# Reordering every engine's instruction sequence, and shortening the buffer rings, in a two-phase adaLN block (selective scan, then two local-attention layers)

## The chip, the cores and the metric

The program runs on one core of a Trainium2 chip. The metric is the device time of one execution in microseconds (us). The kernel before takes 4263.51 us, the median of three executions (4262.46 to 4267.74). The engines of the core are TensorE (PE, whose weight loads are shown apart as PEld), VectorE (DVE), ScalarE (ACT) and GpSimd (POOL); SyncE (SP) only issues transfers here.

## The reference

Input are 16 sequences of 512 tokens by 256 features. The block does two things to each, one behind the other:

```python
h = layernorm(x) * (1 + ca) + sa
xz = h @ W_in.T;  x_ssm, z = split(xz)                 # 2 x 512 features
B = x_ssm @ W_B.T;  C = x_ssm @ W_C.T                  # 16 states
dt = softplus(x_ssm @ W_dt.T + b_dt)
state = exp(dt * A) * state + dt * B * x_ssm           # per feature and state, over 512 tokens
y = (sum over states of state * C) + x_ssm * D
x = x + ga * ((y * silu(z)) @ W_out.T) * sigmoid(gate)
h = layernorm(x) * (1 + cb) + sb
for layer in (0, 1):   # input and output are h
    q, k, v = shift_token(h) @ wqkv[layer]             # 8 heads of 64
    q, k = rotary(l2norm(q) * qs, l2norm(k) * ks)
    h = h + local_attention(q, k, v, window=128) @ wo  # own and previous window
    u = layernorm(shift_token(h)) * lg + lb
    a, g = split(u @ w1 + b1)
    h = h + (a * gelu(g)) @ w2 + b2
out = x + gb * h
```

## The kernel before

**Two phases.** The first, the mixer (tiles with names `a_`), handles the 16 sequences one by one. The second, the stack (names `b_`), makes 32 passes, layer 0 for the 16 sequences and then layer 1.

**The mixer.** The 512 inner features are four blocks of 128 partitions (d = 0 to 3), the 16 states are eight groups of two. One unit is one group of one block, so there are 32 units per sequence, and a tile of a unit has 128 x 1024 float32 (two states by 512 tokens). Units 0 to 15 belong to d = 0 and 1 (even units to d = 0), units 16 to 31 to d = 2 and 3 (even units to d = 2). A unit passes through these steps: `decay` (ACT, L684: the exponential), `bcast` (PE, L565: B spread over partitions into one of two slots; needed for 22 units, whose input DVE makes), `mul` (DVE L737 for those 22, POOL L806 for the other 10), `scan` (DVE, L755), `cmul` (POOL, L813: times C), `sum` (PE, L573: added up in one of two PSUM banks, `a_y_sum0` for even units and `a_y_sum1` for odd). When the last sum of a block is there, `gate` (DVE, L761) reads the bank. `gate` of d = 2 needs sum 30, `gate` of d = 3 needs sum 31, and `skip` (PE, L554) then begins the two banks anew. `bcast` and a `decay` into a slot wait for the scan two units earlier, which read that slot (a `bcast` 1 waits for scan 31 of the sequence ahead). Projections come from PE (L524: `xs`, `z`, `bc`, `dt`), `zcopy` (ACT, L634) clears the bank of `z`. The tiles with C come by DMA (SP, L462): load k fills a ring slot and waits until the products of the pair of units that held that slot are done.

**The stack.** Per pass: q, k and v (PE L1296), norms (ACT L1459 to L1468, DVE L1669 to L1680), rotary (`prot`: POOL L1601 for the cosine half, DVE L1695 for the sine half; `padd` DVE L1701), then per window w (0 to 3) and half `score` (PE L1346), `mask` (DVE L1728, whose second half ends with the row bias, L1734), `exp` (ACT L1506), `rate` (DVE L1745), `pn` (POOL L1628), `pt` (PE L1357 and its copies, DVE L1741 or ACT L1518), `att` (PE L1373), `onorm` (DVE L1759), and then `wo`, layernorm (`add` L1766 and L1770, `cen` L1785, `xn` L1790, `hns` L1652), `ga` (PE L1407), `gelu` (ACT), `gated` (DVE L1802), `hh` (ACT L1571), `hl` (the low part of the hidden values: POOL L1635 for blocks 0 to 4, DVE L1751 for block 5), `wd` (PE L1428, block by block) and `fin` (DVE L1807).

**What sets the order.** No scheduler runs. Each phase has one table of steps: `MIXER_ORDER` (L139) and `ORDER` (L829). An entry `name:i` is step `name` of unit, window or block i; a suffix `-` or `+` shifts it to the sequence before or behind. Each engine goes through the table and carries out, in that order, those steps that it owns (`pipeline`, L433 and L1129); semaphores do the rest. So the table's relative order of two steps of one engine is that engine's order. `BANK_OF` (L842) says which of eight PSUM banks holds each product of the stack. The four constants in L33 are the depths of the rings for decays, states, C tiles and B tiles.

Of the kernel before, what the change touches and what calls it, by code (L numbers as in the profile page):

```python
# [144 lines left out]
bload:9 sum-:15 bcast-:19 dt-:0 zcopy-:3 bcast-:20 cload:3 mul-:19 scan-:16 cmul-:16 skip-:1 decay-:30 bcast-:21
scan-:17 gate-:0 bclow-:0 scan-:18 cload:4 decay-:31 sum-:16 decay:0 sum-:17 bcast-:22 gate-:1 silu-:0 sum-:18
cmul-:17 cmul-:18 scan-:19 mul-:20 bcast-:23 mul-:21 scan-:20 decay:1 soft-:1 scan-:21 mul-:22 sum-:19 bcast-:24
decay:2 sum-:20 bcast-:25 decay:3 cmul-:19 cmul-:20 cload:5 z-:0 z-:1 cmul-:21 mul-:23 decay:4 stat:0 mul-:24 mul-:25
decay:5 decay:6 scan-:22 norm:0 cmul-:22 scan-:23 xcopy:0 cmul-:23 sq2:0 cmul-:24 cmul-:25 sum-:21 z-:2 cmul-:26
x1store:0 bcast-:26 decay:7 z-:3 mod:0 bcast-:27 sum-:22 scan-:24 scan-:25 up:0 mul-:26 sum-:23 cload:6 bcast-:28  # L150
mul-:27 cmul-:27 scan-:26 scan-:27 decay:8 sum-:24 bcast-:29 mul-:28 sum-:25 mul-:29 sum-:26 bcast-:30 mod:1 up:1
sum-:27 scan-:28 bcast-:31 cload:7 scan-:29 dt-:1 mul-:30 sum-:28 cload:8 bcast:0 dtadd-:0 sum-:29 bcast:1 mul-:31
sum-:30 decay:9 cmul-:28 scan-:30 cload:9 scan-:31 cmul-:29 sum-:31 bload:12 decay:10 decay:11 cmul-:30 dev2:0 mul:0
skip:0 scan:0 mul:1 xcopy:1 out:0 bcast:2 gate-:2 gate-:3 xscopy:0 scan:1 decay:12 bcast:3 cload:10 scan:2 h2store:0
# [1883 lines left out]
```

How the kernel before makes its waits and increments, by code:

```python
    def wait_free(self, eng, s, name):  # L81
        n = self.at[name]
        _, bank, lead, *_ = self.uses[n]
        for back, held in ((0, self.uses[:n]), (-1, self.uses), (-2, self.uses)):
            found = [use for use in held if use[1] == bank and self.happens(use, s - lead + back + use[2])]
            if found:
                name, _, before, _, _, released, k = found[-1]
                eng.wait_ge(released.sem, released.at(s - lead + back + before - self.since.get(name, 0), k))
                break
# [1 line left out]
    def wait_full(self, eng, s, name):  # L92
        _, _, _, full, k, _, _ = self.uses[self.at[name]]
        eng.wait_ge(full.sem, full.at(s - self.since.get(name, 0), k))
# [105 lines left out]
    def wait_free(self, eng, s, name):  # L201
        at = next(n for n, use in enumerate(self.uses) if use[0] == name)
        turn = s - self.uses[at][2]
        until = {}
        for bank in self.uses[at][1]:
            for back in (0, -1, -2):
                held = self.uses[:at] if back == 0 else self.uses
                found = [use for use in held if bank in use[1] and self.happens(turn + back + use[2])]
                if found:
                    _, _, lead, signal, k = found[-1]
                    until[signal] = max(until.get(signal, (back + lead, k)), (back + lead, k))
                    break
        for signal, (back, k) in until.items():
            eng.wait_ge(signal.sem, signal.at(turn + back, k))
```

## Time and profile before

| | |
|---|---|
| median of three executions | 4263.51 us |
| the profiled execution | 4263.51 us, span 4261.7 us |
| PE busy | 4046.0 us (95%) |
| DVE busy | 3709.7 us (87%) |
| POOL busy | 2694.5 us (63%) |
| ACT busy | 2678.9 us (63%) |
| last step of the mixer's sequences at | about 1725 us |

The span lies 1.8 us inside the profiled execution's time, and that execution is the median one. Busy shares are means over both phases: the mixer fills about the first 1725 us, the stack the rest.

### The profile page before, as it was taken

The numbers are of one execution on the slowest core, as the hardware profiler recorded it, in microseconds if no ns is written. First come the engines' busy times: TensorE is split into PE (matmuls) and PEld (weight loads), VectorE is DVE, ScalarE is ACT, GpSimd is POOL, SyncE is SP. The second block draws the span as 40 slices with busy tenths as digits, with TensorE's granted clock in tenths as the row PEclk, the third lists the DMA queues.
The fourth block names the chain that finished last, engine by engine and source line by source line (L and its number), as shares of the span: only waits on it lengthen the run. The fifth ranks groups of instructions, "written<-read, shape, count | busy, mean of one in ns | idle before, by whom it ended". The sixth has DMA issues, their size and how long they took to land.

```text
span 4261.7 us, 60079 instructions
## 1 busy us (share of the span) xinstructions
PE 4046.0 (95%) x19614; PEld 2631.5 (62%) x19614; DVE 3709.7 (87%) x5981; ACT 2678.9 (63%) x5767; POOL 2694.5 (63%) x1297
## 2 busy tenths in 40 slices
PE   7999999999999998569999999999999999999997
PEld 4444444444444443357777777777777777777775
DVE  5999999999999999568888888888888888888884
ACT  6776767777766775236566565656656565665654
POOL 3999999999999999344444343444434344443442
PEclk8999999999999999779999999999999999999999
DMA  3333333333333333320000000001110101001000
GB/s 112 115 119 124 120 128 123 127 119 120 124 123 126 119 122 111 108 92 21 26 21 16 31 16 27 20 26 55 53 45 25 32 26 32 30 26 36 21 31 25
DMA packets 118499, 295.02 MB, mean 69 GB/s; under 512 B 21208, under 2 KB 43664, under 8 KB 118192
## 3 DMA queue, kind: packets, MB, share of 16 engines
q1 hardware_dynamic: 116320, 291.15, 20.5%
q8 instruction: 160, 2.62, 0.3%
q14 instruction: 147, 1.20, 0.1%
q10 hardware_dynamic: 1872, 0.05, 0.0%
...
## 4 chain that ended last, share of the span: by engine, by line
PE 50%; DVE 5%; ACT 1%; issue 1%; DMA 1%; POOL 0%; SPq 0%; DVEq 0%
PE b_bank L1296 12%; PE b_bank L1407 12%; PE b_bank L1286 5%; PE b_bank L1373 5%; PE b_bank L1346 5%; PE b_bank L1357 4%; PE b_bank L1428 3%; PE b_bank L1326 3%; DVE b_h_part L1751 2%; DVE b_qk L1680 1%; PE b_bank L1387 1%; PE b_bank L1392 1%; DVE b_probs_t L1741 0%; DVE b_qk_rot L1695 0%; ACT b_probs_t L1518 0%
## 5 line engine op out<-in xcount | busy, mean ns | idle before, releaser
L813 POOL TENSOR_TENSOR a_state<-a_state,a_c_wide 128x1024 f32<-128x1024 f32 x512 | 1195.1, 2369 | 19.5 <-DVE a_state L755 19.5
L573 PE MATMUL a_y_sum<-a_state,a_ident 128*128 128x512 f32 x2048 | 951.4, 597 | 6.8 <-POOL a_state L813 6.8
L1628 POOL TENSOR_TENSOR b_scores<-b_scores,b_row_rate 128x1024 f32<-128x1024 f32 (+1 forms) x256 | 455.4, 1800 | 726.1 <-DVE b_row_rate L1745 726.1
L755 DVE TENSOR_TENSOR_SCAN a_state<-a_decay,a_slot 128x1024 f32<-128x1024 f32 x352 | 788.6, 2270 | 0.7
L1296 PE MATMUL b_bank<-b_w_qkv,b_hx_part 128*128 128x512 f32 x2304 | 634.1, 418 | 34.7 <-DVE b_w_qkv L1830 16.6
L573 PEld LDWEIGHTS a_y_sum<-a_state,a_ident 128*128 128x128 f32 x2048 | 387.3, 191 | 383.2 <-issue 316.9
L1601 POOL TENSOR_TENSOR b_by_cos<-b_qk,b_rotary 128x1024 f32<-128x1024 f32 x128 | 352.9, 2757 | 377.4 <-DVE b_qk L1680 375.4
L1506 ACT ACTIVATE b_scores<-b_scores,b_row_bias 128x256 f32<-128x256 f32 (+1 forms) x1024 | 477.3, 468 | 144.1 <-DVE b_row_bias L1734 144.1
L684 ACT ACTIVATE a_decay<-a_dt,a_neg_a 128x512 f32<-128x512 f32 x704 | 453.9, 710 | 114.6 <-DVE a_state L755 114.2
L1296 PEld LDWEIGHTS b_bank<-b_w_qkv,b_hx_part 128*128 128x128 f32 x2304 | 427.6, 193 | 150.2 <-issue 41.1
L1407 PE MATMUL b_bank<-b_hn_part,b_w 128*128 128x512 f32 x2112 | 513.9, 398 | 6.7 <-DVE b_hn_part L1652 6.7
L1407 PEld LDWEIGHTS b_bank<-b_hn_part,b_w 128*128 128x128 f32 x2112 | 396.1, 189 | 112.3 <-DVE b_hn_part L1652 18.6
L737 DVE TENSOR_TENSOR a_slot<-a_u,a_slot 128x1024 f32<-128x1024 f32 x352 | 417.0, 1213 | 20.1 <-PE a_slot L565 20.1
L1635 POOL TENSOR_TENSOR b_h_part<-b_h,b_h_part 128x512 fp32r<-128x512 f32 x160 | 211.8, 1332 | 322.6 <-ACT b_h_part L1571 322.6
L806 POOL TENSOR_TENSOR a_state<-a_u,a_b_wide 128x1024 f32<-128x1024 f32 x160 | 376.0, 2373 | 3.9 <-PE a_y_sum L573 3.9
L684 ACT ACTIVATE a_slot<-a_dt,a_neg_a 128x512 f32<-128x512 f32 x320 | 208.0, 683 | 248.3 <-DVE a_state L755 248.1
L755 DVE TENSOR_TENSOR_SCAN a_state<-a_slot,a_state 128x1024 f32<-128x1024 f32 x160 | 357.6, 2267 | 2.4 <-ACT a_slot L684 1.7
L1728 DVE CUSTOM_DVE_ANT_0 b_scores<-b_bank,b_squares 128x256 f32<-128x256 f32 (+1 forms) x1024 | 337.7, 385 | 1.7 <-issue 1.7
L1428 PE MATMUL b_bank<-b_h_part,b_w 128*128 128x512 f32 x1088 | 299.7, 409 | 16.5 <-DVE b_h_part L1751 16.5
L1357 PE MATMUL b_bank<-b_squares,b_scores 128*128 128x128 f32 x1792 | 261.5, 278 | 12.9 <-DVE b_qk L1680 6.9
L1459 ACT ACTIVATE b_qk_rot<-b_bank 128x512 f32<-128x512 f32 x256 | 142.7, 596 | 190.0 <-PE b_bank L1296 190.0
L1357 PEld LDWEIGHTS b_bank<-b_squares,b_scores 128*128 128x128 f32 x1792 | 212.0, 142 | 75.4 <-issue 31.3
(201 smaller groups left out, 6882.4 us busy)
## 6 DMA issues: line engine op xcount, KB each, us to landing
a_c_wide<-bc_rows SPq DMA_DIRECT2D x256, 512.0 KB, 3.8
...
```

What stands on the lines that cost most here:

```text
L573: last = nc.tensor.matmul(y_sum[dd][:], ident[:], state[state_ring.slot[q]][:, i, :], start=False, stop=(j == GROUPS - 1 and i == GROUP - 1))
L684: last = nc.scalar.activation(to[:, i, :], dt[slot][:, d, :], ACT.Exp, scale=neg_a[:, d, n:n + 1])
L737: nc.vector.tensor_tensor(slots[q % 2][:], u[slot][:, d, :].unsqueeze(1).to_broadcast([P, GROUP, SEQ]), slots[q % 2][:], ALU.mult).then_in ...
L755: nc.vector.tensor_tensor_scan(flat(h), flat(factor), flat(term), 0.0, ALU.mult, ALU.add).then_inc(scan_done.sem, 1)
L806: nc.gpsimd.tensor_tensor(state[state_ring.slot[q]][:], u[slot][:, d, :].unsqueeze(1).to_broadcast([P, GROUP, SEQ]), b_wide[b_ring.slot[k] ...
L813: nc.gpsimd.tensor_tensor(h[:], h[:], c_wide[c_ring.slot[q // 2]][:], ALU.mult).then_inc(cmul_done.sem, 1)
L1296: last = nc.tensor.matmul(psum.tile(name)[:], x[:, c, w * P:(w + 1) * P].bitcast(F32R), weights[:, c, cols:cols + INNER].bitcast(F32R), st ...
L1357: last = nc.tensor.transpose(psum.tile(name)[:, n * P:(n + 1) * P], scores[w % 2][:, h, blk * WINDOW:(blk + 1) * WINDOW], ident)
L1407: last = nc.tensor.matmul(psum.tile(f"{stem}{m}")[:], weights[:, c, at * P:(at + 1) * P].bitcast(F32R), x[:, c, :].bitcast(F32R), start=(n ...
L1428: last = nc.tensor.matmul(psum.tile(f"wd{m}")[:], weights[:, k, m * P:(m + 1) * P].bitcast(F32R), x[:, held, :].bitcast(F32R), start=(k == ...
L1506: e = nc.scalar.activation(scores[w % 2][:, h, lo:hi], scores[w % 2][:, h, lo:hi], ACT.Exp, bias=row_bias[:, w, h:h + 1], accum_out=row_su ...
L1628: nc.gpsimd.tensor_tensor(probs, probs, row_rate[:, w, at].unsqueeze(2).to_broadcast([P, 4, hi - lo]), ALU.mult)\
```

## The change

The four ring depths are lowered for decays, C and B, and both tables and the bank map are written anew. The steps themselves, their shapes and their count stay.

```diff
-DECAY_SLOTS, STATE_SLOTS, C_SLOTS, B_SLOTS = 4, 6, 3, 3
+DECAY_SLOTS, STATE_SLOTS, C_SLOTS, B_SLOTS = 3, 6, 2, 2
 ...
 MIXER_ORDER = """
-scan-:10 scan-:11 cmul-:6 cmul-:7 scan-:12 scan-:13 bcast-:13 bcmid-:0 xT-:1 xs-:0 xscopy-:3 xs-:1 decay-:19 soft-:0
+sum-:5 bcast-:10 sum-:6 mul-:12 mul-:13 xload:0 bcast-:11 scan-:12 cload-:13 cload-:14 cload-:15 scan-:13 cload:0
 ...
 ORDER = """
-hxs:0 psq:0 mask:1.0 att-:3 score:0.0 prate:0 hxload:0 score:0.1 rate:0 mask:1.1 score:1.0 pss:0 pn:0.1 score:1.1
+ptr-:3 mask:0.0 mask:0.1 att-:3 score:0.0 exp:0 pn:0.0 hxs:0 hxload:0 psq:0 score:0.1 score:1.0 wo:0 mask:1.0 add:0
 ...
 BANK_OF = """
-q_t3:2 k_t3:3 wo0:2 s0_0_0:3 s0_0_1:6 s0_1_0:4 s0_1_1:2 wo1:3 s1_0_0:1 s1_0_1:7 q0:0 k0:4 s1_1_0:5 s1_1_1:6 pt0_0:5
+q_t3:4 k_t3:5 wo0:5 s0_0_0:1 s0_0_1:5 s0_1_0:0 s0_1_1:2 wo1:7 s1_0_0:6 s1_0_1:7 q0:2 k0:6 s1_1_0:3 s1_1_1:4 pt0_0:4
```

**The end of a sequence in the mixer, DVE.** The first two rows are scans 30 and 31 of one sequence, the last ones belong to the sequence behind it, except L761, which is `gate` of d = 2 and d = 3. Before:

```order
L755 SCALAR_TENSOR_TENSOR a_state3<-a_decay1,a_slot0 128x1024
L755 SCALAR_TENSOR_TENSOR a_state4<-a_decay2,a_slot1 128x1024
L737 TENSOR_TENSOR a_slot0<-a_u0,a_slot0 128x1024
L755 SCALAR_TENSOR_TENSOR a_state0<-a_decay0,a_slot0 128x1024
L737 TENSOR_TENSOR a_slot1<-a_u0,a_slot1 128x1024
L761 TENSOR_TENSOR a_u1<-a_y_sum0,a_sz1 128x512
L761 TENSOR_TENSOR a_u1<-a_y_sum1,a_sz1 128x512
L755 SCALAR_TENSOR_TENSOR a_state1<-a_decay1,a_slot1 128x1024
```

Now:

```order
L755 SCALAR_TENSOR_TENSOR a_state4<-a_decay1,a_slot1 128x1024
L737 TENSOR_TENSOR a_slot0<-a_u0,a_slot0 128x1024
L737 TENSOR_TENSOR a_slot1<-a_u0,a_slot1 128x1024
L761 TENSOR_TENSOR a_u1<-a_y_sum0,a_sz1 128x512
L755 SCALAR_TENSOR_TENSOR a_state0<-a_decay0,a_slot0 128x1024
L761 TENSOR_TENSOR a_u1<-a_y_sum1,a_sz1 128x512
L755 SCALAR_TENSOR_TENSOR a_state1<-a_decay1,a_slot1 128x1024
L755 SCALAR_TENSOR_TENSOR a_state2<-a_slot0,a_state2 128x1024
```

The second `mul` of the next sequence and the `gate` of d = 2 now stand ahead of its first scan.

**The same place on PE.** L573 are sums 28 to 31, L565 the spreads 0 and 1 of the next sequence, L554 the skip product. Before:

```order
L573 MATMUL a_y_sum0<-a_state1,a_ident 128x512 x2
L565 MATMUL a_slot0<-a_bc_parts1,a_picks 128x512 x2
L573 MATMUL a_y_sum1<-a_state2,a_ident 128x512 x2
L565 MATMUL a_slot1<-a_bc_parts1,a_picks 128x512 x2
L573 MATMUL a_y_sum0<-a_state3,a_ident 128x512 x2
L573 MATMUL a_y_sum1<-a_state4,a_ident 128x512 x2
L554 MATMUL a_y_sum0<-a_xs1,a_skip_mat 128x512
L554 MATMUL a_y_sum1<-a_xs1,a_skip_mat 128x512
```

Now:

```order
L573 MATMUL a_y_sum0<-a_state1,a_ident 128x512 x2
L565 MATMUL a_slot0<-a_bc_parts0,a_picks 128x512 x2
L565 MATMUL a_slot1<-a_bc_parts0,a_picks 128x512 x2
L573 MATMUL a_y_sum1<-a_state2,a_ident 128x512 x2
L573 MATMUL a_y_sum0<-a_state3,a_ident 128x512 x2
L573 MATMUL a_y_sum1<-a_state4,a_ident 128x512 x2
L554 MATMUL a_y_sum0<-a_xs0,a_skip_mat 128x512
L554 MATMUL a_y_sum1<-a_xs0,a_skip_mat 128x512
```

Spread 1 has moved ahead of sum 29, so sums 29, 30 and 31 all stand behind it.

**The tail of a stack pass, POOL.** L1635 are blocks 2, 3, (then) 4 of `hl`, L1628 is `pn` of window 3 and, in its 4x128 form, of window 0 of the next pass, L1601 is `prot` of window 3. Before:

```order
L1601 TENSOR_TENSOR b_by_cos<-b_qk,b_rotary 128x1024
L1635 TENSOR_TENSOR b_h_part<-b_h,b_h_part 128x512 x3
L1628 TENSOR_TENSOR b_scores<-b_scores,b_row_rate 128x1024 x2
L1635 TENSOR_TENSOR b_h_part<-b_h,b_h_part 128x512
L1601 TENSOR_TENSOR b_by_cos<-b_qk,b_rotary 128x1024
L1628 TENSOR_TENSOR b_scores<-b_scores,b_row_rate 128x4x128 x2
```

Now:

```order
L1601 TENSOR_TENSOR b_by_cos<-b_qk,b_rotary 128x1024
L1635 TENSOR_TENSOR b_h_part<-b_h,b_h_part 128x512 x3
L1628 TENSOR_TENSOR b_scores<-b_scores,b_row_rate 128x1024
L1635 TENSOR_TENSOR b_h_part<-b_h,b_h_part 128x512
L1628 TENSOR_TENSOR b_scores<-b_scores,b_row_rate 128x1024
L1601 TENSOR_TENSOR b_by_cos<-b_qk,b_rotary 128x1024
L1628 TENSOR_TENSOR b_scores<-b_scores,b_row_rate 128x4x128 x2
```

The fourth `hl` now stands between the two halves of `pn`, and `prot` still behind all of them.

**The middle of a stack pass, DVE.** L1728 and L1734 are `mask` of window 2 and its row bias, L1680 the normalised q and k of window 1 (after which POOL can start `prot` of window 1), L1790 `xn`. Before:

```order
L1728 ISA b_scores,b_row_max<-b_bank,b_squares 128x256
L1728 ISA b_row_max 128x1
L1728 ISA b_scores,b_row_max<-b_bank,b_squares 128x256
L1728 ISA b_row_max 128x1
L1734 TENSOR_SCALAR b_row_bias<-b_row_max 128x8
L1680 TENSOR_TENSOR b_qk<-b_bank,b_qk_rate 128x512 x2
L1790 TENSOR_TENSOR b_xc<-b_xc,b_rstd 128x1024
L1741 COPY b_probs_t<-b_bank 128x512
```

Now:

```order
L1680 TENSOR_TENSOR b_qk<-b_bank,b_qk_rate 128x512 x2
L1725 MEMSET b_waiter 128x1
L1728 ISA b_scores,b_row_max<-b_bank,b_squares 128x256
L1728 ISA b_row_max 128x1
L1728 ISA b_scores,b_row_max<-b_bank,b_squares 128x256
L1728 ISA b_row_max 128x1
L1725 MEMSET b_waiter 128x1
L1728 ISA b_scores,b_row_max<-b_bank,b_squares 128x256
L1728 ISA b_row_max 128x1
L1728 ISA b_scores,b_row_max<-b_bank,b_squares 128x256
L1728 ISA b_row_max 128x1
L1734 TENSOR_SCALAR b_row_bias<-b_row_max 128x8
```

L1680 stood behind the row bias; now it stands ahead of the mask and of its bias. The same exchange is made between `mask` of window 1 and `pnorm` of window 0.

## Rows read from the trace of the kernel before

**Rows 1.** busy time by window: mixer, then both layers; us, engines with instruction counts.

```profile
core 0: us, PE busy (x) PEld busy (x) DVE busy (x) ACT busy (x) POOL busy (x), PEclk, DMA share, GB/s
190.00:1640.00 1450.00, 1399.86 (x4166) 684.14 (x4165) 1445.38 (x924) 1022.90 (x1723) 1437.15 (x645) 1.00 0.37 122
2200.00:4100.00 1900.00, 1879.56 (x11692) 1429.64 (x11689) 1605.27 (x3891) 1169.22 (x2974) 805.32 (x430) 1.00 0.09 30
```

**Rows 2.** instructions of one line: `cen2` of the mixer, `add` of layers 0 and 1.

```profile
L773 DVE TENSOR_TENSOR a_xc<-a_x_t,a_work x15: 1189/1193/1195, 189.1 to 1640.3; 128x1024 f32<-128x1024 f32 x15
...
L1770 DVE TENSOR_TENSOR b_rstd<-b_x x15: 1783/1789/1808, 1993.4 to 3033.3; 128x512 f32<-128x512 f32 x15
...
L1770 DVE TENSOR_TENSOR b_rstd<-b_x x10: 1789/1794/1812, 3408.3 to 4086.7; 128x512 f32<-128x512 f32 x10
```

**Rows 3.** waits of DVE, 190 to 1640 us: total, times, longest.

```profile
DVE a_slot L737 <- PE a_slot L565: 3.2, 14, 0.2
```

**Rows 4.** timeline of DVE, 682 to 694.5 us: start, duration, line, count.

```profile
682.75 4.46 DVE L755 TENSOR_TENSOR_SCAN a_state<-a_decay,a_slot 128x1024 f32<-128x1024 f32 x2
687.13 1.21 DVE L737 TENSOR_TENSOR a_slot<-a_u,a_slot 128x1024 f32<-128x1024 f32 x1
688.37 2.29 DVE L755 TENSOR_TENSOR_SCAN a_state<-a_decay,a_slot 128x1024 f32<-128x1024 f32 x1
690.57 1.21 DVE L737 TENSOR_TENSOR a_slot<-a_u,a_slot 128x1024 f32<-128x1024 f32 x1
691.69 1.28 DVE L761 TENSOR_TENSOR a_u<-a_y_sum,a_sz 128x512 f32<-128x512 f32 x2
```

**Rows 5.** timeline of PE in the same stretch.

```profile
685.61 0.60 PE L565 MATMUL a_slot<-a_bc_parts,a_picks 96*128 96x512 bf16 x2
686.04 1.88 PE L573 MATMUL a_y_sum<-a_state,a_ident 128*128 128x512 f32 x4
687.76 0.60 PE L565 MATMUL a_slot<-a_bc_parts,a_picks 96*128 96x512 bf16 x2
688.20 3.62 PE L573 MATMUL a_y_sum<-a_state,a_ident 128*128 128x512 f32 x8
```

**Rows 6.** C tile landings; POOL products with C, 190 to 1640 us.

```profile
DMA to landing us min/median/max: 3.3/3.8/5.9
...
L813 POOL TENSOR_TENSOR a_state<-a_state,a_c_wide x449: 2336/2364/2461, 188.1 to 1639.2; 128x1024 f32<-128x1024 f32 x150
```

**Rows 7.** timeline of PE and ACT, 658 to 663 us.

```profile
659.58 3.35 PE L524 MATMUL a_work<-a_h_part,a_w_in_t 128*128 128x512 f32 x12
...
661.77 0.57 ACT L634 ACTIVATE a_sz<-a_work 128x512 f32<-128x512 f32 x1
```

**Rows 8.** timeline of POOL, DVE and PE near 2413 us; DVE L1751 overall.

```profile
2411.36 1.29 DVE L1680 TENSOR_TENSOR b_qk<-b_bank,b_qk_rate 128x512 f32<-128x512 f32 x2 [0.93 <-ACT b_qk_rate L1468]
...
2413.18 2.37 POOL L1601 TENSOR_TENSOR b_by_cos<-b_qk,b_rotary 128x1024 f32<-128x1024 f32 x1
2413.28 2.83 DVE L1751 TENSOR_TENSOR b_h_part<-b_h,b_h_part 42x512 fp32r<-42x512 f32 x1
...
2416.15 1.20 PE L1428 MATMUL b_bank<-b_h_part,b_w 128*128 128x512 f32 x4 [0.54 <-DVE b_h_part L1751]
...
L1751 DVE TENSOR_TENSOR b_h_part<-b_h,b_h_part x32: 1084/2828/2843, 1967.7 to 4250.9; 42x512 fp32r<-42x512 f32 x32
```

**Rows 9.** timeline of DVE and of POOL, 2425 to 2437 us.

```profile
2426.96 0.17 DVE L1734 TENSOR_SCALAR b_row_bias<-b_row_max 128x8 f32<-128x8 f32 x1
...
2431.56 0.42 DVE L1728 CUSTOM_DVE_ANT_0 b_scores<-b_bank,b_squares 128x256 f32<-128x256 f32 x1
...
2432.02 0.72 DVE L1734 TENSOR_SCALAR b_row_bias<-b_row_max 128x8 f32<-128x8 f32 x1
...
2430.67 2.04 POOL L1628 TENSOR_TENSOR b_scores<-b_scores,b_row_rate 128x512 f32<-128x512 f32 x2 [15.12 <-DVE b_row_rate L1745]
```

**Rows 10.** waits of PE, 2200 to 4100 us.

```profile
PE b_bank L1428 <- DVE b_h_part L1751: 13.7, 25, 0.6
```

More of the change, by code:

```diff
@@ L145 @@
[L145 to L154, printed above, removed]
@@ new lines @@
+cload:1 bload:6 sum-:7 cmul-:10 cload:2 mul-:14 sum-:8 cload:3 decay-:18 bcmid-:0 xs-:0 cmul-:11 cmul-:12 cmul-:13
+cmul-:14 xscopy-:3 cload:4 decay-:19 cload:5 bcast-:12 sum-:9 decay-:20 xs-:1 xs-:2 decay-:21 mul-:15 scan-:14
+scan-:15 mul-:16 cload:6 scan-:16 bload:9 mul-:17 bcast-:13 bcrest-:0 decay-:22 cmul-:15 mul-:18 soft-:0 scan-:17
+decay-:23 bcast-:14 bcast-:15 mul-:19 cload:7 cload:8 gate-:0 bclow-:0 gate-:1 cmul-:16 cmul-:17 decay-:24 zcopy-:0
+cmul-:18 cmul-:19 cmul-:20 decay-:25 sum-:10 zcopy-:1 cstore:0 sum-:11 bc-:0 bcast-:16 scan-:18 zcopy-:2 decay-:26
@@ new lines @@
+decay-:27 cload:9 sum-:12 zcopy-:3 decay-:28 bload:12 scan-:19 bcast-:17 cload:10 decay-:29 cmul-:21 sum-:13 mul-:20
+mul-:21 soft-:1 scan-:20 xs-:3 sum-:14 bcast-:18 scan-:21 decay-:30 mul-:22 mul-:23 sum-:15 mul-:24 mul-:25 dt-:0
+cmul-:22 decay-:31 scan-:22 bcast-:19 bcast-:20 decay:0 skip-:1 scan-:23 decay:1 stat:0 cload:11 bcast-:21
+scan-:24 sum-:16 sum-:17 cmul-:23 bcast-:22 sum-:18 bcast-:23 decay:2 sum-:19 scan-:25 decay:3 cmul-:24 sum-:20
+sum-:21 mul-:26 mul-:27 dtadd-:0 z-:0 scan-:26 decay:4 bcast-:24 scan-:27 x1store:0 silu-:0 z-:1 mul-:28 decay:5
@@ new lines @@
+cload:12 bcast-:25 z-:2 mul-:29 bcast-:26 z-:3 scan-:28 cmul-:25 cmul-:26 cmul-:27 norm:0 cmul-:28 cmul-:29 bcast-:27
+h2store:0 sum-:22 dt-:1 cmul-:30 bcast-:28 scan-:29 sum-:23 bcast-:29 mul-:30 sum-:24 mul-:31 sum-:25 xcopy:0 decay:6
+bcast-:30 scan-:30 bcast-:31 sq2:0 sum-:26 sum-:27 scan-:31 bload+:1 mul:0 sum-:28 decay:7 mul:1 bcast:0 bcast:1
+sum-:29 dev2:0 cmul-:31 decay:8 bcast:2 gate-:2 scan:0 mul:2 gate-:3 scan:1 xcopy:1 scan:2 scan:3 decay:9
+mul:3 mul:4 res:0 sum-:30 mod:0 cmul:0 scan:4 sum-:31 skip:0 decay:10 out:0 bcast:3 res:1 cmul:1 bcast:4 mul:5 out:1
@@ L160 @@
+dtadd-:1 sum:0 bcast:5 up:0 cmul:2 scan:5 xT:0 bcast:6 mod:1 cen2:0 decay:11 up:1 cmul:3 cmul:4 mean2:0 decay:12 mul:6
+sum:1 cmul:5 mul:7 scan:6 bcast:7 mul:8 scan:7 xn2:0 decay:13 bload+:4 scan:8 xscopy:0 sum:2 decay:14 decay:15
+decay:16 xscopy:1 h2:0 scan:9 mul:9 xscopy:2 bcast:8 cmul:6 var2:0 bccopy:0 mul:10 xT:1 hcut:0 mul:11 cmul:7 cmul:8
+sum:3 cmul:9 sum:4 hcut:1 scan:10 scan:11 bcast:9 hT:0 decay:17 bcup:0 hT:1
 """
@@ L840 @@
+gated:2 pk:3 gated:3 hh:1 gated:4 ga:4 padd:2 hh:2 rate:3 pt:2.1 wd:0 x1load:0 gelu:3 gelu:4 hh:3 gelu:5 gated:5 ga:5
+ptc:2 ptr:2 pss:3 outstore:0 psq:3 pq:3 wd:1 pt:2.2 hl:1 wd:2 hh:4 prate:3 pnorm:3 hl:2 hl:3 pn:3.0 hh:5 hl:4 pt:2.3
+wd:3 pt:3.0 wd:4 hl:5 vc:3 pn:3.1 pt:3.1 fin:0 fin:1 wd:5 pt:3.2 prot:3 sum:0 sum:1 turnc:0 padd:3 pt:3.3 turnc:1
+onorm:2 ptc:3 v:3 store:0 att:2 turn:0 turn:1 onorm:3
 """
 BANK_OF = """
[L842 removed]
```

31 lines of the change are left out of this document (9 added, 22 removed).

## The prediction

> **What bounds the kernel now.** I read the page's busy shares first, then the busy time by window, because the two phases have different limits. In the mixer's steady part DVE is busy 1445.4 of 1450 us and POOL 1437.2 [rows 1]: DVE sets the time, POOL follows 0.9 us per sequence behind. In the layers PE is busy 1879.6 of 1900 us and DVE only 1605 [rows 1]: PE sets the time. The clock is granted in full in both (1.00), so no part of the sum is a matter of the clock.
>
> Next the rhythm, from one instruction that occurs once in a sequence or pass. In the mixer L773 starts 15 times from 189.1 to 1640.3 us: 1451.2 / 14 = 103.66 us per sequence. In layer 0, L1770 gives (3033.3 - 1993.4) / 14 = 74.28 us per pass, in layer 1 (4086.7 - 3408.3) / 9 = 75.38 [rows 2]. So the ceilings on any gain are known: DVE idles (1450 - 1445.4) / 14 = 0.33 us per sequence, of which 3.2 / 14 = 0.23 us is a wait for the spread [rows 3], and PE idles 20.4 us in 1900 / 74.8 = 25.4 passes, 0.80 us per pass [rows 1]. The instructions are the same as before, in another order. Whatever is added on DVE in the mixer or on PE in the layers shows in full: 15 times for a sequence's end with another one behind it, 31 times for a pass with another one behind it.
>
> **The mixer: the wait at the gate.** This is the main term. Before, DVE ran scan 31, `mul` 0, scan 0, `mul` 1, the two gates: scans 30 and 31 end at 682.75 + 4.46 = 687.21 us, `mul` 0 starts at 687.13, scan 0 at 688.37, `mul` 1 at 690.57, the gates at 691.69, with nothing idle between [rows 4]. PE ran spread 1 at 687.76, after sum 29 (686.04), and sums 30 and 31 as eight matmuls from 688.20 to 691.82 [rows 5]. Sum 30, the first four, is thus complete at about 690.0, and the gate of d = 2 had 1.7 us in hand.
>
> Now, on DVE, scan 0 (2.29 us) stands behind this gate instead of ahead of it, so DVE comes to it at 687.13 + 2 x 1.12 (from the starts 687.13 to 688.37 and 690.57 to 691.69, 1.12 to 1.24 each) = 689.4 us. And on PE, sum 29 has gone behind spread 1. Spread 1 cannot start before scan 31 has released its slot, at 687.21, wherever it stands; then it takes 0.44 us to the next start (687.76 to 688.20), and two sums of four matmuls lie ahead of the gate in place of one: 3.62 us for eight [rows 5]. Sum 30 is complete at 687.21 + 0.44 + 3.62 = 691.3 us. DVE waits 691.3 - 689.4 = 1.9 us. The gate of d = 3 comes after scan 0, at about 694, when sum 31 (another 1.8 us, 693.1) is done: no second wait. Behind the waiting gate on DVE are scan 0, the second gate and scan 1, and POOL's products with C behind those; POOL has 0.9 us spare per sequence and only follows. PE has (1450 - 1399.9) / 14 = 3.6 us spare and hides its own part. Bounds: 0.9 us if PE's pieces run ahead of spread 1 in the time it waits, 2.4 us if the spread also starts late, as at 687.76 instead of 687.21. I take 1.9.
>
> **The mixer: three smaller ones.** (a) Sum 21 now stands ahead of the first two `z` projections, which are twelve matmuls in 3.35 us with `zcopy` at 661.77 behind them [rows 7]; `zcopy` comes later by a sum, 1.8 us, and on ACT the next decays stand behind it. By the slack of the decays I put 0.2 us on DVE (0 to 0.8). (b) The second half of `dt`, as many matmuls as in rows 7 and so about 3 us, now stands ahead of spread 28, and sum 23 between spreads 28 and 29: `mul` 29 or 30 waits for its spread. 0.3 us (0 to 0.8). (c) The wait for the spread that is there now (0.23) can go or stay: -0.1. Fewer decay slots let ACT run one unit less ahead; ACT is busy 1023 of 1450 us, so it has time to catch up, and I put nothing. Sum: 1.9 + 0.2 + 0.3 - 0.1 = 2.3, rounded down to 2.2 us per sequence, since two waits close together share their cost. 15 x 2.2 = +33 us; bounds 1.5 to 3.2, +23 to +48.
>
> **Two C slots.** A load now waits on SP for the products of the pair two ahead, not three. It has the time of one pair, 2 x 2.364 = 4.73 us, to land, against 3.3 at best, 3.8 in the median and 5.9 at most [rows 6]. Where POOL has other work between two pairs, the time is longer; by the order there are four places per sequence where it has none. The long landings are those of loads issued beside another one, the B tiles above all, and at these four places none is issued beside. I put nothing; at 5.9 it would be up to 1.2 us at a place. The Trainium skill ("DMA: Bandwidth & Descriptors", section "Anatomy of one DMA — SWDGE (gpsimd) path") fits a transfer as about 2.0 us plus its bytes over 436 GB/s: an estimate of 3.2 us for a 512 KB tile alone and 4.4 for two at once. By that too the two slots cost nothing, and the row's fastest landing (3.3) agrees, though this queue is not the one that the page describes.
>
> **The layers: the tail of a pass.** `hl` of block 5 (DVE L1751) runs beside POOL's `prot`: 2413.28 to 2416.11 us beside 2413.18 to 2415.55. In the median of 32 it takes 2.83 us, at its shortest 1.08, and the last block's `wd` waits 0.54 us for it [rows 8], in every pass: 13.7 us in 25 passes [rows 10]. Now the fourth `hl` has moved ahead of the second half of `pn`, and `prot` comes at least one `pn` later; `hl` 5 then meets the end of a `pn` instead of the whole of `prot` and is done in time. Gain: 0.55 us per pass (0 to 0.8, PE's whole idle time).
>
> **The layers: the row bias.** DVE's L1734 takes 0.17 us alone and 0.72 beside POOL's L1628, which ran from 2430.67 to 2432.71; the bias ended at 2432.74 [rows 9]: it waited until POOL was through. Now `pnorm` of windows 0 and 1 comes ahead of `mask` 1 and `mask` 2. POOL's `prot` starts when `pnorm` is done, about 0.5 us behind its end (2412.65 and 2413.18) and runs 2.37 us [rows 8]. The second half of a mask is four heads at 0.35 us (four in 1.4, [rows 9] has one of 0.42 with 0.46 to the bias), so the bias is due 1.5 us behind `pnorm`, when `prot` has 1.4 us to go. It waits about 1.0 to 1.4 us, twice per pass, and the `exp`, the rates, `pt` and DVE's next copies are all behind it. PE works on from other windows in between; of 2 x 1.2 us I take a third as seen by PE, +0.75 us per pass (0 to 2.0).
>
> The Trainium skill ("SBUF — State Buffer", section "Who interferes with whom") says that a DVE instruction with both inputs in SBUF, or a `tensor_scalar` in its two-port mode, shares a port pair with GpSimd, that whoever issues first holds it for the whole instruction, and that the other blocks altogether. Rows 9 agree with that. By the rule the bias would end with `prot`, 1.4 us late each time; the sum above goes by the rows.
>
> Layer 1 has 1.1 us more per pass than layer 0, and its extra steps move too (the turns now ahead of the last transposition); I see as much for as against. Stack: -0.55 + 0.75 = +0.2 us, x 31 = +6 us; bounds -0.8 and +1.2 us, -25 to +37.
>
> **The sum.** The profiled execution took 4263.51 us with a span of 4261.7, and is itself the median: 4263.5 + 33 + 6 = 4302.5; I say 4302. Fill and drain of the two phases also change, by a few us either way.
>
> **Rivals.**
> - *B, the bias costs nothing.* PE has other windows' work, so the late `exp` is hidden, while the tail's wait goes: 4263.5 + 33 - 17 = 4279. For it: PE waits almost only for L1751 [rows 10]. Against it: PE's idle time is so small that it has no queue of finished inputs to live from.
> - *C, the C ring.* The four tight loads land late by 0.3 us each: +1.2 us per sequence on POOL, which has 0.9 spare already used by DVE's wait; 15 x 1.2 = 18, 4320. For it: the maximum of 5.9 us [rows 6]. Against it: the median.
> - *D, the other side: faster.* PE reaches its floor in the layers: the whole 0.8 us of idle time goes, 31 x 0.8 = -25 us, and the gate's wait is short since PE does sum 29 while it waits for scan 31 (0.9 instead of 1.9 us, and the small ones don't show): +14. That gives 4253; it decides once the mixer adds less than 1.1 us per sequence. Against it: an engine carries out its instructions in order, and spread 1 stands ahead of sum 29.
> - *E, POOL's operations hold DVE longer.* `hl` 5 is now held by `pn` and then by `prot` too, so that `wd` 5 waits 1 us more, or both biases show in full: about +1 us per pass, 4263.5 + 33 + 31 = 4328.
>
> **Chances.** Forecast 0.52, B 0.17, C 0.10, D 0.10, E 0.11. The likeliest case alone ranges from 4284 to 4320. The range of 8 in 10 leaves out most of D below and half of E above: 4262 to 4328. A measurement of this kernel tells about 0.2%, 8.5 us, from no change. Faster by more than that: most of D, 0.08. Within: the rest of D, and cases where the mixer's wait is small and B holds, 0.12. Slower: 0.80.
>
> **What would show it.** Right: L773 every 105.5 to 106.5 us; DVE's waits in the mixer led by L761 for L573, 1.9 us each, once per sequence; L1751 well under 2.8 us in the median and PE's wait for it gone; L1734's median above 1 us in windows 1 and 2; L1770 every 74 to 75.5 us. Wrong: no wait at L761 with the rhythm at 103.7 (the main term falls); POOL waits for a DMA at L813 (C); L1428 still waits for L1751 (the tail's gain falls, E); the layers' rhythm under 73.7 us (D).

## The result, and the profile after

The changed kernel takes 4311.77 us (median of four, 4310.83 to 4315.74), the kernel before 4265.62 in the same series: 1.011 times as long, 95% interval 1.0093 to 1.0128. The forecast was 4302 us, in a range from 4262 to 4328. The profiled execution took 4316.54 us, 4.8 more than that median, with a span of 4314.5, 52.8 us more span than before.

The busy time by window, for the mixer's steady part and the layers (columns as in [rows 1]):

```profile
198.00:1681.00 1483.00, 1398.36 (x4150) 681.25 (x4149) 1443.20 (x919) 1018.80 (x1718) 1431.98 (x642) 1.00 0.36 119
2250.00:4150.00 1900.00, 1877.44 (x11626) 1422.32 (x11626) 1573.36 (x3872) 1163.37 (x2976) 760.70 (x431) 1.00 0.09 30
```

DVE now idles 39.8 of 1483 us where it idled 4.6 of 1450; PE in the layers is where it was (22.6 us idle of 1900 in place of 20.4). The rhythm, by the same instructions as [rows 2]:

```profile
L773 DVE TENSOR_TENSOR a_xc<-a_x_t,a_work x15: 1194/1195/1196, 197.4 to 1688.4; 128x1024 f32<-128x1024 f32 x15
...
L1770 DVE TENSOR_TENSOR b_rstd<-b_x x15: 691/692/693, 2040.4 to 3081.2; 128x512 f32<-128x512 f32 x15
...
L1770 DVE TENSOR_TENSOR b_rstd<-b_x x10: 691/692/693, 3457.5 to 4136.7; 128x512 f32<-128x512 f32 x10
```

The mixer goes from 103.66 to (1688.4 - 197.4) / 14 = 106.50 us per sequence, layer 0 from 74.28 to 74.34 us per pass, layer 1 from 75.38 to 75.47. By the first and the last start of these lines the span divides without a rest: up to the first L773, the fill, 197.4 us in place of 189.1 (+8.3), fifteen sequences 1589.5 in place of 1551.5 (+38.0), the hand-over +0.5, the 31 pass distances 2301.0 in place of 2295.1 (+5.9), the end +0.1. The fifteenth sequence is a shorter one in both kernels (100.3 and 98.5 us), so the mixer's +38.0 is 14 times 2.84 less 1.8.

What DVE waits for in the mixer, to be set beside [rows 3]:

```profile
DVE a_u L761 <- PE a_y_sum L573: 25.2, 14, 1.9
DVE a_slot L737 <- PE a_slot L565: 9.0, 17, 1.4
DVE a_state L755 <- ACT a_slot L684: 3.8, 14, 0.3
```

The first line was absent before; it alone makes 25.2 / 14 = 1.8 us per sequence. The place itself, DVE and then PE, one sequence's end (compare [rows 4, 5]):

```profile
703.22 4.46 DVE L755 TENSOR_TENSOR_SCAN a_state<-a_decay,a_slot 128x1024 f32<-128x1024 f32 x2
707.59 2.34 DVE L737 TENSOR_TENSOR a_slot<-a_u,a_slot 128x1024 f32<-128x1024 f32 x2
711.81 0.69 DVE L761 TENSOR_TENSOR a_u<-a_y_sum,a_sz 128x512 f32<-128x512 f32 x1 [1.88 <-PE a_y_sum L573]
712.42 2.28 DVE L755 TENSOR_TENSOR_SCAN a_state<-a_decay,a_slot 128x1024 f32<-128x1024 f32 x1
714.61 0.66 DVE L761 TENSOR_TENSOR a_u<-a_y_sum,a_sz 128x512 f32<-128x512 f32 x1
```

```profile
706.71 0.60 PE L565 MATMUL a_slot<-a_bc_parts,a_picks 96*128 96x512 bf16 x2
707.73 0.60 PE L565 MATMUL a_slot<-a_bc_parts,a_picks 96*128 96x512 bf16 x2 [0.43 <-DVE a_state L755]
708.17 5.32 PE L573 MATMUL a_y_sum<-a_state,a_ident 128*128 128x512 f32 x12
```

Scans 30 and 31 end at 707.68. Spread 1 has waited for that and starts at 707.73; sums 29, 30 and 31 follow it as twelve matmuls from 708.17 on. Eight of them take 3.62 us [rows 5], so sum 30 is there at 711.79. DVE has both `mul` done at 709.93 and waits 1.88 us.

In the layers, DVE's two lines of the prediction and PE's waits (first columns as in [rows 8, 10]):

```profile
L1751 DVE TENSOR_TENSOR b_h_part<-b_h,b_h_part x32: 778/1356/1373, 2014.9 to 4303.7; 42x512 fp32r<-42x512 f32 x32
...
L1734 DVE TENSOR_SCALAR b_row_bias<-b_row_max x103: 170/1053/1105, 2250.4 to 4149.5; 128x8 f32<-128x8 f32 x103
```

```profile
PE b_bank L1407 <- DVE b_hn_part L1652: 14.0, 25, 0.6
```

The last `hl` takes 1.36 us in place of 2.83, and PE no longer waits for it. In its place PE waits for the low part of the normalised input (L1652), 14.0 / 25 = 0.56 us per pass, which is what it waited for L1751 before. And L1770 itself, one of the layernorm's additions on DVE, takes 0.69 us in place of 1.79 (the rows above and [rows 2]), which the prediction didn't have: 1.1 us of DVE's time per pass.

### The profile page after: what moved, and what is told of

It reads as the page before. It is cut to its first block, busy times and chain, and to the rows that moved or that the text cites. A ratio compares the mean times of both kernels' runs of the same rounds, so it can differ in the third digit from the quotient of the medians.

```text
span 4314.5 us, 60081 instructions
## 1 busy us (share of the span) xinstructions
PE 4052.9 (94%) x19614; PEld 2629.3 (61%) x19614; DVE 3679.9 (85%) x5981; ACT 2672.4 (62%) x5767; POOL 2639.3 (61%) x1297
## 4 chain that ended last, share of the span: by engine, by line
PE 34%; DVE 14%; issue 4%; ACT 4%; DMA 1%; SPq 0%; POOL 0%; DVEq 0%; ACTq 0%
PE b_bank L1407 12%; PE b_bank L1428 6%; PE b_bank L1296 5%; PE b_bank L1357 3%; PE b_bank L1373 3%; PE b_bank L1286 3%; ACT b_scores L1506 2%; DVE b_scores L1728 2%; DVE b_qk L1680 2%; DVE b_qk_rate L1669 2%; PE b_bank L1326 1%; PE b_bank L1346 1%; DVE b_qk_rot L1695 1%; DVE b_qk_rot L1701 1%; DVE b_xc L1785 1%
## 5 line engine op out<-in xcount | busy, mean ns | idle before, releaser
L1628 POOL TENSOR_TENSOR b_scores<-b_scores,b_row_rate 128x1024 f32<-128x1024 f32 (+1 forms) x256 | 426.5, 1682 | 969.6 <-DVE b_row_rate L1745 969.6
L573 PE MATMUL a_y_sum<-a_state,a_ident 128*128 128x512 f32 x2048 | 942.3, 598 | 0.7 <-POOL a_state L813 0.6
L1296 PE MATMUL b_bank<-b_w_qkv,b_hx_part 128*128 128x512 f32 x2304 | 661.7, 426 | 35.2 <-DVE b_w_qkv L1830 16.2
L573 PEld LDWEIGHTS a_y_sum<-a_state,a_ident 128*128 128x128 f32 x2048 | 387.1, 191 | 401.0 <-issue 342.4
L1601 POOL TENSOR_TENSOR b_by_cos<-b_qk,b_rotary 128x1024 f32<-128x1024 f32 x128 | 336.7, 2631 | 252.0 <-DVE b_qk L1680 249.9
L737 DVE TENSOR_TENSOR a_slot<-a_u,a_slot 128x1024 f32<-128x1024 f32 x352 | 417.2, 1213 | 24.6 <-PE a_slot L565 24.5
L1635 POOL TENSOR_TENSOR b_h_part<-b_h,b_h_part 128x512 fp32r<-128x512 f32 x160 | 205.2, 1291 | 267.9 <-ACT b_h_part L1571 267.9
L1728 DVE CUSTOM_DVE_ANT_0 b_scores<-b_bank,b_squares 128x256 f32<-128x256 f32 (+1 forms) x1024 | 337.5, 385 | 3.4 <-issue 3.4
L1802 DVE SCALAR_TENSOR_TENSOR b_h<-b_bank,b_b_1a,b_gelu 128x512 f32<-128x512 f32 x192 | 143.4, 747 | 167.5 <-POOL b_h_part L1635 64.3
L565 PE MATMUL a_slot<-a_bc_parts,a_picks 96*128 96x512 bf16 x704 | 213.4, 386 | 69.0 <-DVE a_state L755 67.6
```

Of the source, the lines that this page charges most:

```text
L573: last = nc.tensor.matmul(y_sum[dd][:], ident[:], state[state_ring.slot[q]][:, i, :], start=False, stop=(j == GROUPS - 1 and i == GROUP - 1))
L737: nc.vector.tensor_tensor(slots[q % 2][:], u[slot][:, d, :].unsqueeze(1).to_broadcast([P, GROUP, SEQ]), slots[q % 2][:], ALU.mult).then_in ...
L1296: last = nc.tensor.matmul(psum.tile(name)[:], x[:, c, w * P:(w + 1) * P].bitcast(F32R), weights[:, c, cols:cols + INNER].bitcast(F32R), st ...
L1628: nc.gpsimd.tensor_tensor(probs, probs, row_rate[:, w, at].unsqueeze(2).to_broadcast([P, 4, hi - lo]), ALU.mult)\
L1728: last = nc.vector.tensor_tensor_reduce(out=scores[w % 2][:, head, lo:hi], in0=psum.tile(f"s{w}_{g}_{h}")[:, at + lo:at + hi], in1=mask[:, ...
```

## The experiments

Two kinds of figures are kept apart: times are medians beside runs of the kernel before on the same chip, and rhythms are read from the profile of each run. Where a distance from one sequence to the next is given as regular, it is the one that most sequences of the run have: 103.65 us in the kernel before, 106.25 in the changed one, in which three of 14 sequences take 107.4: in these the clock of PE fell (see the last section). The first two runs divide the change.

**The changed mixer alone** (`ORDER` and `BANK_OF` as before).

> The changed mixer (its table and its ring depths) with the stack's tables of before. Theory (the mixer carries nearly all): the span is 4261.7 + 46.8, about 4308 us: 8.3 us of fill, 38 us over the 15 rhythms, rhythm 106.5 us per sequence; the layers stay at 74.28 and 75.38. Rival (the stack's change carries a good part, and only the hand-over between the phases hides it): under 4295 us.

Measured: 4313.4 us beside 4267.3, ratio 1.0104 (1.009 to 1.0118), span 4311.1. L773 from 196.8 to 1786.1, so 1589.3 us for fifteen sequences. The mixer carries the result.

**The changed stack alone** (`MIXER_ORDER` and the ring depths as before).

> The mixer of before with the changed stack tables. Theory: +6 us, about 4268 us of span, rhythms of 74.34 and 75.45 us, PE waiting 0.56 us per pass for the high part of the normalised input (L1652) and no more for L1751: two changes of half a microsecond that cancel. Rival (the stack's new order is better in itself and loses only because the mixer feeds it late): 4255 us or less.

Measured: 4271.56 us beside 4267.3, ratio 1.0011 (1.0002 to 1.002), rhythm of layer 0 (3040.3 - 1999.3) / 14 = 74.36. The pass distances sum to 2301.2 us, 6.1 more than before, 2.4 of them in the last pass. As forecast (but L1652, for which PE waits, writes the low part of the normalised input, not the high part). One thing was not: this run has the mixer of before, and yet its first L773 is at 194.7 us and not 189.1. In four other runs with that mixer's first part it lies at 190.7 to 192.3, with the changed mixer at 195.1 to 198.4. So of the fill's 8.3 us about half is the change's and the rest is scatter of this stretch.

**Scan 0 ahead of the gate** (the changed kernel, DVE only).

```diff
-gate-:2 scan:0 mul:2 gate-:3 scan:1
+scan:0 gate-:2 mul:2 gate-:3 scan:1
```

> The changed kernel with scan 0 moved on DVE ahead of the gate of d = 2. Theory (the gate waits for sum 30, which is there 1.9 us after DVE comes to it, and scan 0 takes 2.3 us): DVE's wait at L761, 1.8 us per sequence, goes; the rhythm falls from 106.5 to 104.7, the span by 27 us to 4287. Rival (the rhythm is set by another engine, POOL or PE, and DVE's wait is only where it shows): the wait moves to another line and the rhythm stays above 106.

Measured: 4305.16 us, ratio 1.0089 (1.0075 to 1.0103), span 4302.3: 12 us under the changed kernel's profiled span, 8 us less by the medians beside the kernel before (+37.8 in place of +46.1), and not 27. The regular distance is 105.2 us, 1.05 less, and seven of 14 sequences take 106.3, each with a fall of PE's clock. In the diff `mul` 2 is POOL's, so on DVE the two gates follow each other. DVE's timeline at the same place:

```profile
705.48 2.34 DVE L737 TENSOR_TENSOR a_slot<-a_u,a_slot 128x1024 f32<-128x1024 f32 x2
707.72 2.28 DVE L755 TENSOR_TENSOR_SCAN a_state<-a_decay,a_slot 128x1024 f32<-128x1024 f32 x1
709.92 0.67 DVE L761 TENSOR_TENSOR a_u<-a_y_sum,a_sz 128x512 f32<-128x512 f32 x1
711.42 0.69 DVE L761 TENSOR_TENSOR a_u<-a_y_sum,a_sz 128x512 f32<-128x512 f32 x1 [0.83 <-PE a_y_sum L573]
```

The gate of d = 2 no longer waits, but the gate of d = 3, now directly behind it, waits 0.83 us for sum 31, the last of the same chain. Neither theory had it: the first is right about the wait and wrong about what stands behind it.

**Sum 29 ahead of spread 1** (the changed kernel, PE only).

```diff
-bcast:0 bcast:1 sum-:29
+bcast:0 sum-:29 bcast:1
```

> The changed kernel with spread 1 put back behind sum 29 on PE. Theory (in-order PE holds sum 29 behind a spread that waits for scan 31): PE does sum 29 in that wait, sum 30 is there one sum (1.8 us) earlier, L761's wait falls to 0.1 to 0.3 us, the rhythm to about 104.8, the span to about 4289. Rival (sums 29 and 30 come late because POOL's products do): L761 waits 1.8 us as before, and PE waits for L813.

Measured: 4304.09 us, ratio 1.009 (1.0076 to 1.0104), span 4299.0, every distance 105.7 us where 104.8 was expected; no sequence has a fall of the clock.

```profile
703.32 1.21 DVE L737 TENSOR_TENSOR a_slot<-a_u,a_slot 128x1024 f32<-128x1024 f32 x1
705.22 1.23 DVE L737 TENSOR_TENSOR a_slot<-a_u,a_slot 128x1024 f32<-128x1024 f32 x1 [0.69 <-PE a_slot L565]
706.94 0.69 DVE L761 TENSOR_TENSOR a_u<-a_y_sum,a_sz 128x512 f32<-128x512 f32 x1 [0.49 <-PE a_y_sum L573]
```

The wait at the gate falls from 1.88 to 0.49 us (0.1 to 0.3 was expected), and a wait of 0.69 us comes up at `mul` 1: without a scan between the two `mul`, DVE is at the second before spread 1 is there. POOL was not the cause (the rival).

**Both, with the whole order of before at that place.**

```diff
-mul:0 sum-:28 decay:7 mul:1 bcast:0 bcast:1 sum-:29 ... gate-:2 scan:0 mul:2 gate-:3
+mul:0 sum-:28 decay:7 bcast:0 sum-:29 bcast:1 ... scan:0 mul:1 gate-:2 mul:2 gate-:3
```

> The changed kernel with the order of before at the end of a sequence, on both engines: DVE scan 31, mul 0, scan 0, mul 1, both gates; PE spread 1 behind sum 29. With one of the two edits each the rhythm fell from 106.25 to 105.2 and 105.65. Theory (both gates wait for a chain on PE; two sums and one scan must stand ahead of them): no wait at L761, and 103.65 + 0.3 + 0.34 - 0.23 + 0.27 = 104.3 us per sequence, the span 28 us under the changed kernel's. Rival (the changed order wants other sums late, so that POOL's products are late too): 105 us or more.

Measured: 4299.61 us beside 4265.3, ratio 1.008 (1.0067 to 1.0094), span 4294.8. Eight of 14 distances are 104.6 us, 0.3 over the theory's 104.3; the other six are 106.3, for a reason of their own: L737 waits six times 1.37 us there (13.1 us in all, less 14 times 0.34), see the last section. They bring the mean to 105.3 us, which is over the rival's bound too, but not by the rival's cause; and by the medians the gain on the changed kernel is 12 us, not 28.

```profile
DVE a_slot L737 <- PE a_slot L565: 13.1, 20, 1.4
DVE a_state L755 <- ACT a_slot L684: 3.8, 14, 0.3
DVE a_u L761 <- PE a_y_sum L573: 1.9, 6, 0.3
```

**The reverse: the kernel before with the two exchanges alone.**

```diff
-sum-:29 bcast:1 mul-:31 sum-:30
+bcast:1 sum-:29 mul-:31 sum-:30
-scan:0 mul:1 xcopy:1 out:0 bcast:2 gate-:2 gate-:3
+mul:1 xcopy:1 out:0 bcast:2 gate-:2 scan:0 gate-:3
```

> The kernel before with the two exchanges alone: on PE spread 1 ahead of sum 29, on DVE scan 0 behind the gate of d = 2. Theory: a wait of 1.9 us at L761 in every sequence and nothing else in the mixer; rhythm 103.65 + 1.9 = 105.5 us, the span +28 us, 4290. Rival (the two exchanges cost only together with the rest of the new order): under 4275 us.

Measured: 4295.09 us beside 4265.27, +29.8 us, ratio 1.0068 (1.0054 to 1.0082). Every distance is 105.5 us.

```profile
DVE a_u L761 <- PE a_y_sum L573: 24.5, 13, 1.9
DVE a_slot L737 <- PE a_slot L565: 3.2, 14, 0.2
```

This is the cleanest run of the study: the kernel before, two steps exchanged, the wait of 24.5 / 13 = 1.88 us and nothing else new. The two exchanges are enough for the main term. Of the 30.7 us that this profile's span lies above that of the kernel before, 25.9 are 14 times 1.85; most of the rest is the fill (+3.2) and the hand-over (+2.8), two stretches that differ as much between other runs.

**The smaller terms.** Both runs start from the kernel with scan 0 ahead of the gate.

```diff
-dt-:1 cmul-:30 bcast-:28 scan-:29 sum-:23 bcast-:29
+cmul-:30 bcast-:28 scan-:29 sum-:23 bcast-:29 dt-:1
```

> The changed kernel with scan 0 ahead of the gate of d = 2, and on PE the second half of dt moved behind spread 29. To be compared with the kernel that has only the first edit. Theory (the projections hold spreads 28 and 29 back): DVE's wait at L737 for L565 falls from 0.64 to about 0.25 us per sequence, the rhythm by 0.4 us, the span by 6 us. Rival (a spread comes late for another reason, as its slot's scan): no difference.

```diff
-sum-:21 mul-:26 mul-:27 dtadd-:0 z-:0 ... z-:1
+mul-:26 mul-:27 dtadd-:0 z-:0 ... z-:1 sum-:21
```

> The changed kernel with scan 0 ahead of the gate of d = 2, and on PE sum 21 moved behind the first two z projections. Theory (zcopy 0 comes a sum later and holds the next decay back): DVE's wait at L755 for a decay (0.27 us per sequence) goes, the rhythm falls by 0.27 us, the span by 4 us against the kernel with the first edit alone. Rival (that wait comes from a ring slot or from POOL's order): it stays.

Measured: 4306.0 and 4306.5 us, against 4305.2 without these edits: neither gains. In the first, DVE's waits for a spread are gone but for one (1.2 us), and the scans wait for PE's sums to release a state tile instead, 12.5 / 14 = 0.9 us. The regular distance rises from 105.2 to 105.7 us; the total stays because PE's clock falls in one sequence in place of seven. In the second, the wait for the decay is gone, as the theory says, and the waits for spreads have risen from 14.3 to 18.3 us in all, 0.28 per sequence, as much as the decay's 0.27; the regular distance stays at 105.2.

```profile
DVE a_state L755 <- PE a_y_sum L573: 12.5, 14, 1.2
...
DVE a_slot L737 <- PE a_slot L565: 1.2, 1, 1.2
```

```profile
DVE a_slot L737 <- PE a_slot L565: 18.3, 35, 1.4
```

So each of the two waits goes with the edit that was held to cause it, and another comes in its place.

**The ring depths of before** with the changed tables.

> The changed kernel with the ring depths of before (4, 6, 3, 3 for decays, states, C and B). Theory (two C slots and three decay slots are enough for the new order, POOL never waits for a tile): the same within 3 us, 4314 us of span. Rival (fewer slots cost 0.3 to 1 us per sequence, or part of the 8.3 us of the fill): 4297 to 4308 us.

Measured: 4315.68 us beside 4266.6, ratio 1.0117 (1.01 to 1.0134), rhythm 106.44 as with the shallow rings, and the same three waits of DVE within 0.1 us in total. The shallower rings cost nothing that shows.

**The tail: the fourth `hl` moved, in the kernel before.**

```diff
-wd:1 pn:3.1 pt:2.2 prate:3 hh:4 hl:4 wd:2
+wd:1 pt:2.2 prate:3 hh:4 hl:4 pn:3.1 wd:2
```

> The kernel before with one change: on POOL, hl of block 4 ahead of the second half of pn of window 3. Theory (DVE's hl of block 5 then meets the end of pn and not prot): L1751's median falls from 2.83 to about 1.4 us, PE's wait for it (0.55 us per pass) goes, the span falls by up to 17 us, to 4245. Rival (the second half of pn comes late, and the transpositions of window 3 with it, which PE then waits for): 4262 us or more.

Measured: 4251.62 us beside 4268.72, ratio 0.9966 (0.9952 to 0.9979), span 4249.7. This version beats both kernels. The stretch of [rows 8] in this kernel, and layer 0's rhythm:

```profile
2412.79 1.29 POOL L1635 TENSOR_TENSOR b_h_part<-b_h,b_h_part 128x512 fp32r<-128x512 f32 x1 [4.50 <-ACT b_h_part L1571]
...
2414.05 1.89 POOL L1628 TENSOR_TENSOR b_scores<-b_scores,b_row_rate 128x1024 f32<-128x1024 f32 x1
2414.14 2.34 DVE L1751 TENSOR_TENSOR b_h_part<-b_h,b_h_part 42x512 fp32r<-42x512 f32 x1
...
2415.90 2.84 POOL L1601 TENSOR_TENSOR b_by_cos<-b_qk,b_rotary 128x1024 f32<-128x1024 f32 x1
...
2416.54 1.20 PE L1428 MATMUL b_bank<-b_h_part,b_w 128*128 128x512 f32 x4
```

```profile
L1751 DVE TENSOR_TENSOR b_h_part<-b_h,b_h_part x32: 684/2340/2344, 1971.5 to 4239.0; 42x512 fp32r<-42x512 f32 x32
...
L1770 DVE TENSOR_TENSOR b_rstd<-b_x x15: 1789/1797/1802, 1996.8 to 3029.8; 128x512 f32<-128x512 f32 x15
```

L1751 runs beside the second half of `pn`, ends at 2416.48, and `wd` starts at 2416.54 with no wait of PE. It takes 2.34 us and not the 1.4 that was expected, since `pn` too holds it up, but it starts early enough. The rhythm is 73.79 us, 0.49 less.

**The masks back ahead of the norms**, with the mixer of before and the changed stack.

```diff
-pss:0 pnorm:0 pq:0 pk:0 pn:0.1 resload:0 score:1.1 mask:1.1 ... pnorm:1 var:0 mask:2.1
+mask:1.1 pss:0 pnorm:0 pq:0 pk:0 pn:0.1 resload:0 score:1.1 ... mask:2.1 pnorm:1 var:0
```

> The mixer of before and the changed stack tables, with the masks of windows 1 and 2 (second half, with the row bias) put back ahead of the norms whose end starts POOL's prot. To be compared with the kernel that has the mixer of before and the changed stack tables alone. Theory (the bias waits for POOL and makes exp and hns late): L1734's median falls from 1.05 us to under 0.4, PE's wait for L1652 (0.56 us per pass) goes or halves, the span falls by 9 to 17 us, to 4251 to 4259. Rival (PE's wait for L1652 comes from the order of xn behind prot on DVE, and the bias's lateness is hidden): the bias is short and the time stays within 3 us.

> The mixer of before and the changed stack tables, with one exchange undone: the second half of the mask of window 2, with its row bias, ahead of the norm of window 1 (and so of POOL's prot). In the run with the changed stack alone DVE has no idle time from that bias (2235.18 us, 1.09 us long) to the input cut (L1652) that PE then waits 0.55 us for. Theory (the bias's wait for POOL, 0.92 us, is what PE waits for): the bias takes 0.17 us, L1652's wait goes, the layers' rhythm falls by 0.55 us, the span by 17 us. Rival (the norm and prot of window 1 come 1.5 us later instead, and PE waits for q and k of window 1, as it did when both masks were moved): the same or slower.

Measured: both masks moved, 4334.26 us, ratio 1.0157 (1.0143 to 1.0171). Only that of window 2, 4310.0 us, ratio 1.0107 (1.0093 to 1.012). Both are slower than the changed stack as it is (1.0011), by about 63 and 39 us between medians. The first run met neither of its two expectations: the bias is short, but PE's wait for L1652 stays and the time doesn't. PE waits there 33.8 / 25 = 1.35 us per pass for L1770, which takes 2.37 us in place of 0.69, and 1.0 us for L1680; in the second run only the wait for L1680 is left. DVE and POOL around the bias of window 2, first in the changed stack, then with its mask moved; and PE's waits there:

```profile
2232.46 1.29 DVE L1680 TENSOR_TENSOR b_qk<-b_bank,b_qk_rate 128x512 f32<-128x512 f32 x2
...
2233.82 2.41 POOL L1601 TENSOR_TENSOR b_by_cos<-b_qk,b_rotary 128x1024 f32<-128x1024 f32 x1 [3.88 <-DVE b_qk L1680]
...
2235.18 1.09 DVE L1734 TENSOR_SCALAR b_row_bias<-b_row_max 128x8 f32<-128x8 f32 x1
```

```profile
2235.80 0.17 DVE L1734 TENSOR_SCALAR b_row_bias<-b_row_max 128x8 f32<-128x8 f32 x1
2235.91 1.29 DVE L1680 TENSOR_TENSOR b_qk<-b_bank,b_qk_rate 128x512 f32<-128x512 f32 x2
2237.95 0.69 DVE L1741 COPY b_probs_t<-b_bank 128x512 f32<-128x512 f32 x1 [0.75 <-PE b_bank L1357]
```

```profile
PE b_bank L1357 <- DVE b_qk L1680: 25.4, 25, 1.0
PE b_bank L1407 <- DVE b_hn_part L1652: 14.3, 25, 0.6
```

In the changed stack the bias ends at 2236.27 us, 0.04 behind POOL's `prot`; with the mask ahead it takes 0.17 us. So it did wait for POOL. But L1680, now behind the mask, ends at 2237.20, and PE waits 1.0 us for it before the transpositions of window 1, at 2237.26; and the wait for L1652 stays at 0.57 us. In the kernel before that norm came behind the mask too, at no cost. The order of DVE and the bank map were written together; the exchange can't be undone alone. The rival of the second run held.

## Why the prediction was right, and where it missed

**What bounds the kernel.** Right. Neither phase had room for a gain beyond 0.33 and 0.8 us per period, and every wait added on DVE in the mixer showed in full. One sentence of it didn't hold for the kernel that came of the change: that no part of the sum is a matter of the clock. PE's clock fell in three of the changed kernel's 14 sequences, at 1.1 us each, 3.3 us in all.

**The wait at the gate: 1.9 us forecast, 1.88 measured**, in the changed kernel and again in the reverse experiment. The step failed only in its remark on the gate of d = 3: it doesn't wait because scan 0 lies between, and once that is moved away it waits 0.83 us.

**The smaller terms: +0.3 us forecast, +0.7 measured in a regular sequence and 1.0 in the mean.** DVE waits 0.27 us for a decay (0.2 forecast, its cause shown) and 0.34 at a `mul` where 0.23 stood before, so 0.1 more (+0.3 for the projections and -0.1 for the old wait forecast; cause shown). A further 0.3 us per sequence in the regular distance of 106.25 is in no wait. Added up over DVE's 66 instructions of a sequence, the overlaps of neighbours (`mul` at 707.59 with 2.34 us for two) make 5.16 us before and 4.95 now, and the durations 108.49 and 108.58: about 0.2 us is overlap lost and 0.1 is longer instructions. Two more runs with this mixer divide it otherwise (overlap 5.05 and 5.00, durations 108.69 and 108.64). That each wait breaks one overlap of 0.1 us fits this, but was not tried by itself. The mean has 0.24 us more, the three sequences of 107.4. The step "two waits close together share their cost", by which the sum was rounded down to 2.2, shows nowhere.

**Fifteen times 2.2 is 33; measured 38.0.** The fill, put down as a few us either way, was 8.3 us later in the compared executions, about half of it by the change. So the two profiles lie 52.8 us apart where 39 were forecast, the medians 46.1: the changed kernel's profiled execution is 4.8 us above its median, that of before 2.1 us below. The 10 us between 4302 and 4311.8 are those 7 and the 2.1 us by which the forecast started low. How they divide between the mixer's term (5 us short in the profiles) and the fill can't be told more closely than single executions scatter.

**Two C slots: nothing forecast, nothing measured.** DMA landings are 3.3 to 5.3 us, and no wait of POOL for a tile shows among its lines. Case C is out, and the run with the old depths shows it directly. Cases B and E, which put the stack at -17 and +31 us, are out by the run with the changed stack alone.

**The tail: 0.55 us per pass forecast to be gained.** The mechanism is shown, in isolation (0.49 us per pass, 15 us between the first and the last pass, 17 between the medians); in the changed kernel the wait goes, but another of the same size stands in its place.

**The row bias: +0.75 us forecast, and the stack's total of +6 met.** Here the total is right and one term's cause is open, so that the total may be met by luck. The delay of 0.9 us at two biases per pass is measured; it is under the forecast's 1.0 to 1.4, because `prot` starts 0.07 us behind the end of L1680 and not 0.5. But the kernel before had two delayed biases too: its four take 0.17, 0.72, 0.17 and 0.57 us in a pass (windows 0 to 3), those of the changed kernel 0.17, 1.06, 1.09 and 0.17. The change adds 0.9 us per pass and not 2 x 1.2; the prediction counted both from the undisturbed 0.17, though [rows 9] show the 0.72. What follows from it is not shown: the changed stack loses about what the tail gains, and PE waits for L1652. DVE has no idle time in the 7 us between that bias and L1652, which speaks for the bias; but with the bias short PE's wait stayed, since other waits had come in. Another cause in the rewritten middle of the pass is not excluded. A run that moves the bias alone, with the masks and norms where they are, would decide it, and was not made.

**Case D** (faster) failed as argued: PE does nothing past a spread that waits. Its other half, a stack without PE's idle time, came only in part, and in another kernel: the isolated tail edit gains 0.49 of the 0.80 us.
